# Moving the double tiles of a mixture-of-experts pipeline forward, with two weight units split twice in one job

## What is computed

```python
x = x + tanh(g_xattn[0]) * xattn(layernorm(x), ctx_1024, itok, Wq, Wkv, Wo)
# _L0_ffn_ref(x, ...) on layernorm(x):
top_v, top_i = top_k(softmax(x @ gate_w.T), 2)
for e in range(8):
    h = silu(x @ w1[e] + b1[e])        # 256 -> 1024
    y = h @ w2[e] + b2[e]              # 1024 -> 256
    out = out + y * comb_w[..., e:e + 1]
x = x + tanh(g_ffn[0]) * out
```

## Time and profile before

| what | us |
|---|---|
| median of 3 runs | 329.94 |
| lowest and highest of them | 327.1, 330.24 |
| the profiled execution, its own time | 326.77 |
| the profiled execution, span of its instructions | 324.9 |
| mean granted TensorE clock in it | 0.982 |

### The profile page before, as it was taken

One profiled execution on the slowest core, in us unless ns is written; L12 is line 12 of the kernel. 1 busy time (PEld: TensorE's weight loads), 2 busy tenths in 40 slices (PEclk: granted clock), 3 DMA queues, 4 the chain that ended last, 5 costly groups with the idle time before them and its releaser, 6 DMA issues.

```text
span 324.9 us, 10613 instructions
## 1 busy us (share of the span) xinstructions
PE 294.6 (91%) x3513; PEld 245.6 (76%) x3513; DVE 239.3 (74%) x581; ACT 192.6 (59%) x560; POOL 194.0 (60%) x222
## 2 busy tenths in 40 slices
PE   8698989999989778999998999979999799989960
PEld 7457778899879677888787877968779687887830
DVE  4658998888988987887786686857767678856440
ACT  2442467767555726866675857757667658755520
POOL 3376798997775127257564576546775546762443
PEclk9999999999999979999999999999999999999995
DMA  7799999999999963326454254633464234545233
GB/s 247 244 323 417 405 418 414 401 415 407 344 391 373 383 220 95 68 51 82 71 82 70 49 82 73 91 61 67 67 94 77 49 68 70 95 73 59 26 40 34
DMA packets 48441, 57.64 MB, mean 177 GB/s; under 512 B 22232, under 2 KB 42560, under 8 KB 46208
## 3 DMA queue, kind: packets, MB, share of 16 engines
q0 software_dynamic: 8896, 25.84, 30.6%
q1 hardware_dynamic: 34144, 27.69, 28.3%
q10 hardware_dynamic: 5344, 3.37, 3.3%
HBM read 42.93 MB, written 9.76 MB: 162 GB/s over the span
## 4 chain that ended last, share of the span: by engine, by line
PE 26%; issue 24%; POOL 18%; DVE 14%; ACT 9%; ACTq 4%; DVEq 2%; DMA 2%; POOLq 1%
PE ps L1306 9%; ACT w_parts L934 4%; POOL sel L565 4%; PE ps L1321 4%; DVE sel L1804 3%; POOL w_parts L565 3%; POOL w_parts L597 2%; POOL sel L597 2%; ACT sel L987 2%; PE ps L1097 2%; DVE xn L1845 2%; DVE xn L1848 2%; PE ps L1010 2%; PE ps L1322 2%; DVE sel L1806 2%
## 5 line engine op out<-in xcount | busy, mean ns | idle before, releaser
L1306 PE MATMUL ps<-sel,w_parts 128*128 128x128 f16 (+1 forms) x1824 | 131.5, 214 | 1.4 <-issue 0.8
L1306 PEld LDWEIGHTS ps<-sel,w_parts 128*128 x1824 | 110.9, 98 | 28.9 <-issue 3.1
L677 POOL DMA_INDIRECT out<-sel x34 | 54.2, 1595 | 69.9 <-DMA out<-sel 26.4
L987 ACT ACTIVATE sel<-ps,b1T 128x128 f32<-128x128 f32 (+1 forms) x304 | 79.2, 375 | 6.5 <-PE ps L1306 4.9
L1321 PE MATMUL ps<-w_parts,sel 128*128 x210 | 78.3, 379 | 0.2 <-DVE sel L1806 0.2
L1791 DVE SCALAR_TENSOR_TENSOR w_parts<-w_parts (+1 forms) x32 | 39.2, 1227 | 31.9 <-ACT w_parts L934 25.1
L1322 PE MATMUL ps<-w_parts,sel 128*128 x210 | 57.2, 272 | 0.0
L669 POOL DMA_INDIRECT sel<-tokens_split,sel x34 | 38.9, 1143 | 20.6 <-DVE sel L1749 10.9
L1806 DVE SCALAR_TENSOR_TENSOR sel<-sel 128x512 f16<-128x512 f32 x68 | 47.1, 692 | 2.3
L968 ACT ACTIVATE sel<-xn,sel 128x256 f32<-128x256 f32 x30 | 15.3, 508 | 40.6 <-DVE xn L1848 37.4
L934 ACT ACTIVATE w_parts<-w_parts (+1 forms) x32 | 33.5, 1049 | 9.0 <-issue 5.7
(11 more groups left out here) (257 smaller groups left out, 491.3 us busy)
## 6 DMA issues: line engine op xcount, KB each, us to landing
w_parts<-in_L_ffn_w SPq DMA_DIRECT2D x16, 1024.0 KB
out<-xs SPq DMA_DIRECT2D x16, 128.0 KB
tokens_split<-xsplit ACTq DMA_DIRECT2D x13, 128.0 KB
xs<-in_x ACTq DMA_DIRECT2D x2, 512.0 KB, 6.8
xs<-in_x SPq DMA_DIRECT2D x2, 512.0 KB, 7.5
near_rows<-w_parts SPq DMA_DIRECT2D x4, 256.0 KB, 9.3
xs<-in_L_ffn_b SPq DMA_DIRECT2D x1, 1024.0 KB
sel<-tokens_split,sel POOLq DMA_INDIRECT x34
```

Source lines behind the costliest of these rows:

```text
L677: pool.indirect_dma_start(out_rows, bass.IndirectOffsetOnAxis(column, 0), y_sb[q % 4][rows, :], None, compute_op=ALU.add).then_inc(s["scat ...
L987: silu = act.activation(h32[n][:, cols], ps_h[n][:, cols], ACT.Silu, bias=own[:, c:c + 1], scale=1.0 / (X_SCALE * W_SCALE))
L1306: mm = pe.matmul(ps_h[n][:, to], w, xT[n][:, a, side * wide:side * wide + wide], start=(i == 0), stop=(i == len(products) - 1))
```

## The change

The list of jobs puts double tile n behind full tile 6, 11, 16 and 21. The double tiles are then jobs 7, 13, 19 and 25; the number and kinds of jobs are the same. The plan of the splits becomes a table: one unit in each job from 0 to 25, and a second one in jobs 9 and 15, so unit 14 is split in job 9 and unit 21 in job 15. Until job 8 unit q + 4 is split in job q, in jobs 10 to 15 unit q + 5, from 16 to 25 unit q + 6; jobs 26 and 27 have none. On ScalarE the second unit comes right behind the first, on VectorE behind `halves(q+1, 0)` and ahead of the sum of job q-1.

```diff
     for f in range(N_FULL):
         JOBS.append((False, f))
-        if f % 6 == 0 and 0 < f < SURE:
-            JOBS.append((True, f // 6 - 1))
+        if f % 5 == 1 and 5 < f < 22:
+            JOBS.append((True, f // 5 - 1))
...
-    assert NT == NL and JOBS.index((True, PAIRS - 1)) == ALWAYS - 4 and JOBS[ALWAYS] == (False, SURE)
+    assert NT == NL and JOBS.index((True, PAIRS - 1)) == ALWAYS - 7 and JOBS[ALWAYS] == (False, SURE)
...
     UNITS = 4 * E
+    SPLITS = {q: [q + 4 + (q > 9) + (q > 15)] for q in range(UNITS - 6)}
+    for q in (9, 15):
+        SPLITS[q].append(SPLITS[q][0] + 1)
+    assert [u for q in SPLITS for u in SPLITS[q]] == list(range(4, UNITS))
...
                 if live(-2) and q < ALWAYS:
                     rows_scaled(q - 2)
-                if 0 <= q < UNITS - 4:
-                    split_weights(q + 4)
+                for u in SPLITS.get(q, []):
+                    split_weights(u)
...
                 if live(0):
                     with filled(dve, tiles, q):
                         halves(q, n, 1)
-                if 0 <= q < UNITS - 4:
-                    split_weights(q + 4)
+                if q in SPLITS:
+                    split_weights(SPLITS[q][0])
...
                 if live(1):
                     with filled(dve, tiles, q + 1):
                         halves(q + 1, m, 0)
+                if len(SPLITS.get(q, [])) > 1:
+                    split_weights(SPLITS[q][1])
                 if q + 1 < ALWAYS and live(-1):
                     (pair_out if is_pair(q - 1) else rows_out)(q, k, m)
```

## The result

The changed kernel takes 332.42 us (median of 15 runs, 330.4 to 335.08), the kernel before 327.98 us in the 15 runs beside it: ratio 1.0135, 95% interval 1.010 to 1.017. It is 1.35% slower. The forecast was 0.5% more, 331.6 us. The time lies in the range of 327.4 to 334.5 us; "the same" had the chance of 0.65, and what happened is "slower by over 1%", which had 0.25. The profiled execution took 334.23 us (span 332.5), 1.8 us more than the median, where that of before was 1.2 us under its median. So the two profiles lie 7.6 us apart in span, and the timed medians 4.4; the 3 us between them belong to these two executions.

The account below looks back on a forecast made before the run. Bound: a ring of DVE and ACT beside PE, and queued scatters at the end. A 3.4 us gain against 4.7 us lateness, with the scatter queue, made the span 1.7 us longer: 331.6 us, range 327.4 to 334.5.

Parts of the forecast that it names:

- the ring: Expert phase: DVE and ACT wait for each other, not for PE; their lateness makes PE's pair_rows stalls, 4.6 us before.
- the doubled splits: Second units in jobs 9 and 15: each makes DVE and ACT 1.8 us later, 3.6 together; bounds 0.95 and 2.4 each.
- the place of the stalls: PE's waits at pair_rows for the sums of double tiles 0, 1 and 2: about 1.3, 2.8 and 3.4 us.
- The wait for unit 29: Step 24, double tile 3's up-projection: PE waits 1.5 us for the last unit's low part, bounds 0 and 2.5.
- The rival: PE's clock falls behind double tile 2's stall, costing 1.7 us of PE's work: 333.3 us, chance 0.20.
- a clock below 1.00 after 246: Sign in the after profile, PE's granted clock after 246 us: below 1.00 would show the forecast wrong.
- the pause of 0.8 us is saved in part: PE's pause where four register loads met a double tile's down-projection: between 0 and 0.8 us saved, taken as 0.4.
- PE's lateness: PE at the end: 3.9 us late through double tile 2, plus 1.5 waiting, less 0.4; taken as 4.7.
- The scatters' price: Queue from double tile 3's first scatter at 285.0: four intervals of 4.25 us and five of 4.12, ending at 322.6.
- the rival that had 0.12: Scatters stay behind: intervals of 4.7 us while gathers run, queue 2 us longer at the end, 333.6 us, chance 0.12.
- The net: Last scatter: 3.4 us gained by the earlier last double tile, eaten by 4.7 us of lateness; span 1.7 us longer.

Follow-up runs that it names:

- e4: The kernel before, with ACT's high part of the split ahead of the scaling of job q-2 in every step: 322.74 us, ratio 0.9826.
- e3: The changed kernel, ACT's high part ahead of the scaling in every step, DVE splitting both units together in jobs 9 and 15: 321.95 us, ratio 0.9795.
- e1: The changed kernel's plan of splits with the old order of jobs (double tiles at 7, 14, 21, 28): 332.06 us, ratio 1.0118.
- e2: The changed kernel; in jobs 9 and 15 ACT splits the first unit ahead of the scaling, DVE both ahead of halves(q+1, 0): 329.34 us, ratio 1.0038.
- e5: The changed kernel with 24 idle matmuls ahead of PE's wait in pair_rows of double tiles 1 and 2: 332.14 us, ratio 1.014.
- e6: The changed kernel, with DVE's second split in jobs 9 and 15 moved behind the sum of job q-1: 330.32 us, ratio 1.0072.
- e7: The changed kernel's order with six units split ahead of the jobs, not four, and no doubled job: 334.16 us, ratio 1.022.

## Why the prediction was right, and where it was off

**The number: luck has a part in it.** 331.6 us was worked out on a median of 329.94 us of three runs; beside the changed kernel the kernel before took 327.98. So the forecast was 1.7 us more and the measurement is 4.4 us more. On the 329.94 a change of 1.35% gives 334.4, just inside the upper end of the range.

**Right: the ring bounds the phase.** e4 shows it for the kernel before, e3 for the new order: a change that takes no work away and only gives the splits another place in ACT's queue (in e3 two of DVE's too) gains 1.7 to 2.1% against the kernel before.

**Right: the doubled splits.** 1.8 us each were forecast. The first measured 6.7 - 4.9 = 1.8, the second 1.3 to 1.4 after its register load. By timed runs, the plan alone costs 1.2% (e1), and hiding it gives back 1.0% (e2), 3.2 us against 3.6.

**Right: the place of the stalls.** Forecast 1.3, 2.8 and 3.4 us; measured 0.4, 2.4 and 2.7. Double tile 2's sum ended at 249.44 + 0.42 = 249.9, forecast 249.5.

**The wait for unit 29: right in kind, not seen in the changed kernel.** Forecast 1.5 us with bounds 0 and 2.5. It is hidden in the changed kernel, 0.7 us in e2, and 2.1, 2.1 and 2.2 us in e5, e6 and e7, where the clock does not hide it.

**The clock: right that it falls, its price open.** The rival had 0.20, and a clock below 1.00 after 246 was named as a sign of being wrong. It fell behind double tile 2, where it was said, by the 1.7 us that were said. But the rival added the 1.7 us to a sum that had the wait for unit 29 in it, and in the changed kernel the fall stands in place of that wait. In e5 and e6 both come, one after the other: the wait ahead of step 24 and a fall behind it. No run keeps the changed kernel's splits where they are and is without a fall, so what the fall costs in time isn't shown. Nor do all executions look alike: of the 15 of the changed kernel, the five with the lowest mean clock (0.974 to 0.976) took 332.9 to 335.1 us and the five with the highest (0.983 to 0.986) 330.4 to 332.2; the profiled one is of the first.

**Wrong: "the pause of 0.8 us is saved in part".** It was to be 0.4 us less and became 0.8 more (1.6 in three places). With the new order these pauses are 1.3 to 1.9 us in two to five places (changed kernel, e2, e3, e5, e6, e7), with the old order 0.8 to 1.0 in one (before, e1, e4), counted from 130 us on. The new order has pauses at other steps; which instruction makes them was not tried.

**PE's lateness, added up.** The scaling of the last job but one begins at 319.18 and not at 311.94, and 0.8 us of the difference are there at the first matmul of step 0 (128.59 and 127.75). The other 6.4 us stand against 4.7 forecast. Up to the end of the stall for double tile 2 it is 3.4 us (forecast 3.9). After that stall it is 3.0 (forecast 1.5 - 0.4 = 1.1): 1.7 of the clock, 0.8 of the pauses and 0.5 that no row names.

**The scatters' price.** Forecast: nine intervals from 285.0 to 322.6, 4.2 us each. Measured 4.5 in the profiled execution of the changed kernel, near the 4.7 of the rival that had 0.12, and 4.4 in e2; but 4.1 to 4.2 in e3, e5, e6 and e7, with the same order. In these four the last scatter but one goes 0.8 us after the scaling of its data, so there the queue was empty and the data set the end. The 4.5 are worth 3.2 us in one execution; that the timed median lies 3 us nearer to before than that execution says that they are not usual.

**What is left between 1.005 and 1.0135.** These are 4.4 - 1.7 = 2.7 us. The pauses, the unnamed 0.5 us, the clock and, in some executions, the scatters are the candidates; how they share it the timed runs do not tell.

**The net.** The new order does shorten the queue at the end, by 3.1 us between e4 and e3, but the time of e3 is only 0.3% shorter, not clear of noise. In the changed kernel what it saves is eaten by PE's lateness, as forecast; e1 without the new order and the changed kernel with it differ by 0.2% with intervals that overlap.

Both kernels are beaten by e3 (321.95 us) and e4 (322.74 us), which cannot be told apart. e4 is one statement moved.

## What to carry to other kernels

An engine at 91% with few waits can still be held by a ring of two others that pace each other: look at whether the intervals of a slower engine are the same from step to step while it waits for its partner, and not for the busy one. Before work is doubled in a step, look where in the in-order queues it stands: behind the result that the partner waits for it costs half, inside the partner's own idle time nothing. Losses on the same stretch are not to be added: between double tile 2 and step 24 PE lost as much with a slow clock and no wait for weights as with the wait and the full clock. And look at the clock over the whole phase after such a trial, not only where it fell before: here the fall came back one wait later.

## What was not expected of the hardware

From 128 us to the end of PE's work, each fall of the clock in these traces came behind a long wait of PE: behind 2.06 us (e6, for unit 29), 2.13 (e2), 2.14 (e5, for unit 29), 2.71 (changed), 4.02 (e1) and 5.61 (e7) a stretch of 2 us had a clock of 0.50. But behind 2.09 us (e6, double tile 2), 2.21 (e7, for unit 29) and 2.44 (changed, double tile 1) it stayed at 1.00, and the earlier trace rows have a fall at 114 to 120 where the longest single wait was 1.45 us. So the length of the last wait alone does not decide. The falls behind 2.13, 2.14 and 2.71 us cost about 1.7 us of PE's work each. The Trainium skill (TensorE: Matmul & The Clock Gate, Part 1: The HAM clock gate) has the throttled state as the default that activity lifts; that every fall came behind a wait agrees with it. One interval between two adding scatters was 6.4 us, where its neighbours took 4.0 and 4.3; no run here shows why.
